# Stencil steps of a fused kernel: the row-neighbour products go into TensorE's PSUM sum, which becomes the new field

## The reference

```
ux = 0.5 * (jnp.roll(g, 1, axis=2) - jnp.roll(g, -1, axis=2))
vy = 0.5 * (jnp.roll(g1, 1, axis=3) - jnp.roll(g1, -1, axis=3))
...
D = 1.0 / (1.0 + 2.0 * Bx + 2.0 * By)
...
for _ in range(K):
    prev = h
    h = D * (c0 * h0 - 2.0 * E * h + cm_x * jnp.roll(h, 1, axis=2) + cp_x * jnp.roll(h, -1, axis=2) + cm_y * jnp.roll(h, 1, axis=3) + cp_y * jnp.roll(h, -1, axis=3))
    h = h + D * (2.0 * DT) * fsrc
    h0 = prev
return jax.nn.relu(_bn(h, out_gamma, out_beta, out_mean, out_var))
```

## Time and profile before

| what | value |
|---|---|
| median of 3 runs | 951.99 us (950.78 to 953.58) |
| the profiled execution, first to last instruction (its span) | 951.3 us |
| mean granted TensorE clock, as a share of full speed | 0.959 |
| matmul records, DVE instructions, POOL instructions | 3950, 671, 240 |

### The profile page before, as it was taken

How to read it: one execution, slowest core, us unless ns; L and a number is a source line. 1 busy time by engine, 2 the same in 40 slices (tenths; PEclk the granted TensorE clock), 3 DMA queues, 4 the chain that set the end, 5 groups by cost and what they waited for, 6 DMA issues and landing times. The chain is left out here.

```text
span 951.3 us, 10709 instructions
## 1 busy us (share of the span) xinstructions
PE 771.3 (81%) x3950; PEld 512.7 (54%) x3950; DVE 798.0 (84%) x671; ACT 552.9 (58%) x953; POOL 513.2 (54%) x240
## 2 busy tenths in 40 slices
PE   3999998987666778688799899898766677877895
PEld 2444443444366667678655444344435566866773
DVE  5899886269899898999989978725889999999983
ACT  3664332126758898889477433212484779888932
POOL 2005995020478697778410299901126969867841
PEclk8899999999899899999899999989998999999998
DMA  3000000000535345355200200000033445545521
GB/s 108 1 0 0 0 0 1 0 1 0 166 111 177 130 179 185 127 178 178 67 1 0 67 1 0 0 0 1 1 99 110 156 156 177 190 144 177 160 86 22
DMA packets 33296, 75.03 MB, mean 79 GB/s; under 512 B 15708, under 2 KB 15844, under 8 KB 33248
## 3 DMA queue, kind: packets, MB, share of 16 engines
q1 hardware_dynamic: 31840, 73.09, 23.2%
q0 software_dynamic: 320, 1.05, 0.5%
q10 hardware_dynamic: 1088, 0.26, 0.1%
HBM read 70.71 MB, written 2.62 MB: 77 GB/s over the span
## 5 line engine op out<-in xcount | busy, mean ns | idle before, releaser
L370 POOL TENSOR_TENSOR arena<-arena 128x1024 f32<-128x1024 f32 x127 | 300.7, 2381 | 92.7 <-DVE arena L1705 81.8
L1705 DVE TENSOR_TENSOR_SCAN arena<-arena,ps 128x1024 f32<-128x1024 f32 x128 | 289.4, 2280 | 19.2 <-ACT arena L931 11.4
L931 ACT ACTIVATE arena<-arena 128x128 f32<-128x128 f32 (+3 forms) x408 | 152.4, 448 | 86.2 <-DVE arena L1632 75.3
L931 ACT ACTIVATE arena<-arena,Amat 128x1024 f32<-128x1024 f32 x128 | 146.0, 1145 | 61.1 <-DVE arena L1705 60.4
L618 PE MATMUL ps<-mat,arena 128*128 128x128 f32 x1016 | 136.4, 279 | 3.3 <-POOL arena L370 2.5
L577 PE MATMUL ps<-mat,arena 128*128 128x128 f32 x560 | 79.1, 287 | 73.3 <-DVE arena L1705 58.6
L618 PEld LDWEIGHTS ps<-mat,arena 128*128 128x128 f32 x1016 | 119.0, 145 | 6.0 <-POOL arena L370 3.7
L577 PEld LDWEIGHTS ps<-mat,arena 128*128 128x128 f32 x560 | 63.3, 142 | 90.6 <-DVE arena L1705 74.2
L737 PE MATMUL ps<-arena,mat 128*128 128x512 f32 x240 | 106.3, 592 | 0.0
L931 ACT ACTIVATE arena<-ps 128x1024 f32<-128x1024 f32 (+2 forms) x65 | 56.1, 873 | 82.5 <-PE ps L449 23.6
L480 PE MATMUL ps<-arena,diag 128*128 128x512 f32 x180 | 83.0, 618 | 2.4 <-DVE ps L1543 2.4
(11 more groups left out here) (205 smaller groups left out, 1291.6 us busy)
## 6 DMA issues: line engine op xcount, KB each, us to landing
arena<-c_rows SPq DMA_DIRECT2D x128, 512.0 KB, 4.0
out<-arena SPq DMA_DIRECT2D x28, 64.0 KB, 2.3
xres<-x POOLq DMA_DIRECT2D x4, 256.0 KB, 5.5
xres<-x SPq DMA_DIRECT2D x4, 256.0 KB, 4.1
arena<-arena SPq DMA_DIRECT2D x4, 252.0 KB
convw<-conv_w SPq DMA_DIRECT2D x1, 576.0 KB
c_rows<-ROWS SPq DMA_DIRECT2D x4, 128.0 KB, 1.9
mat<-mats SPq DMA_DIRECT2D x1, 448.0 KB, 3.9
```

What stands on the lines that cost most here:

```text
L370: tt(HC[s % 2], HS[s % 2], CB[s % 4], ALU.mult).then_inc(S("hc"), 1)
L931: return nc.scalar.activation(out_, in_, func, bias=bias, scale=scale, accum_out=accum_out)
L1705: nc.vector.tensor_tensor_scan(HS[q], DA[q], PS[q][:, :], 0.0, ALU.mult, ALU.add).then_inc(S("scan"), 1)
```

## The change

PE adds two more terms: `R` and `XY` each go through the identity matrix into the same sum. The sum in PSUM is then the whole new field. POOL's add into `G1` and DVE's `new_h` are gone. The tile that holds the sum is the next step's field, and the tile that held the old field is seeded with the source for the next sum: the two tiles swap roles (`field_ps`). ACT copies the new field from PSUM to `hw` (`keep_field`) and no longer from `hw` to PSUM. The product with `P0` is made once per step in `products`, and steps 0 and 1 share the first one, which POOL makes; it lies in `g` or in `G1` by turns (`kept_product`). All loops over steps are written out instead of being hardware loops. At the end ACT's relu reads the sum's PSUM tile.

```diff
+        def field_ps(k, t):
+            return PS[2 * k + 1 - t % 2]
+
+        def kept_product(k, t):
+            return A[k]["g" if t < 2 or t % 2 else "G1"]
...
-                with pool.Fori(0, STEPS) as t:
+                for t in range(STEPS):
                     for k in range(2):
...
-                        pool.wait_ge(S("a_Q6"), 2 * h + k + 1)
-                        pool.wait_ge(S(f"a{k}_act"), 3 * it + 1)
-                        tt(img(a["R"]), img(a["Pmx"]), hw[:, :, 0:32], ALU.mult)
+                        if t == 0:
+                            pool.wait_ge(S("a_Q6"), 2 * h + k + 1)
+                        pool.wait_ge(S(f"a{k}_hw"), 2 * it + 2)
+                        tt(img(a["R"]), img(a["Pmx"]), hw[:, :, 0:32], ALU.mult).then_inc(S(f"a{k}_x"), 1)
                         tt(img(a["XY"]), img(a["G"]), hw[:, :, 2:34], ALU.mult).then_inc(S(f"a{k}_x"), 1)
-                        pool.wait_ge(S(f"a{k}_x"), 2 * it + 1)
-                        tt(a["G1"][:, :], a["R"], a["XY"], ALU.add).then_inc(S(f"a{k}_x"), 1)
...
+            def stencil_sum(h, k, t):
+                a, it, mix = A[k], STEPS * h + t, field_ps(k, t + 1)
+                pe.wait_ge(S(f"a{k}_seed"), 6 * h + t + 2)
+                pe.wait_ge(S(f"a{k}_g"), 4 * h + max(t, 1))
+                for n in range(2):
+                    mm(half(mix, n), ident, half(kept_product(k, t), n), start=False, stop=False, skip_group_check=True)
+                for name, count, mname, src in [("c", 2 * it + 1, "roll_up", "Pmy"), ("c", 2 * it + 2, "roll_down", "sden"), ("e", it + 1, "ident", "X"),
+                                                ("x", 2 * it + 1, "ident", "R"), ("x", 2 * it + 2, "ident", "XY")]:
+                    pe.wait_ge(S(f"a{k}_{name}"), count)
+                    for n in range(2):
+                        last = mm(half(mix, n), mt(mname), half(a[src], n), start=False, stop=(src == "XY"), skip_group_check=True)
+                last.then_inc(S(f"mix{k}"), 1)
...
+            def keep_field(h, k, t):
+                hw, field = wrapped(A[k]["hw"]), img(field_ps(k, t))
+                act.wait_ge(S(f"mix{k}"), STEPS * h + t)
+                av(hw[:, :, 1:33], field, ACT.Identity).then_inc(S(f"a{k}_hw"), 1)
+                act.wait_ge(S(f"a{k}_hw"), 2 * (STEPS * h + t) + 1)
                 av(hw[:, :, 0:1], hw[:, :, 32:33], ACT.Identity)
...
+            def seed(h, k, t):
+                if t == 0:
+                    act.wait_ge(S("a_Sc1" if k else "a_Sc"), h + 1)
+                if t >= 2:
+                    act.wait_ge(S(f"a{k}_g"), 4 * h + t)
+                av(field_ps(k, t + 1)[:, :], A[k]["Sc"], ACT.Identity).then_inc(S(f"a{k}_seed"), 1)
...
-                    act.wait_ge(S(f"a{k}_h"), (STEPS + 1) * h + STEPS + 1)
-                    av(img(PS[2 * k + 1]), wrapped(a["hw"])[:, :, 1:33], ACT.Relu, par[:, 4:5], par[:, 5:6]).then_inc(S("a_bnout"), 1)
+                    act.wait_ge(S(f"mix{k}"), STEPS * h + STEPS)
+                    av(field_ps(k, STEPS - 1)[:, :], field_ps(k, STEPS)[:, :], ACT.Relu, par[:, 4:5], par[:, 5:6]).then_inc(S("a_bnout"), 1)
...
+                else:
+                    dve.wait_ge(S(f"a{k}_hw"), 2 * (STEPS * h + t) + 1)
                 tt(img(a["Pmy"]), img(a["Kx"]), field, ALU.mult).then_inc(S(f"a{k}_c"), 1)
                 tt(img(a["sden"]), img(a["Ky"]), field, ALU.mult).then_inc(S(f"a{k}_c"), 1)
...
                 tt(img(a["X"]), img(a["Pe"]), field, ALU.mult).then_inc(S(f"a{k}_e"), 1)
...
-            def new_h(h, k, t):
-                a = A[k]
-                dve.wait_ge(S(f"mix{k}"), ONE + 2 * (STEPS * h + t + 1))
-                dve.wait_ge(S(f"a{k}_x"), 2 * (STEPS * h + t + 1))
-                tt(wrapped(a["hw"])[:, :, 1:33], img(PS[2 * k]), img(a["G1"]), ALU.add).then_inc(S(f"a{k}_h"), 1)
...
+                if 1 <= t < STEPS - 1:
+                    tt(img(kept_product(k, t + 1)), img(a["P0"]), field, ALU.mult).then_inc(S(f"a{k}_g"), 1)
...
+                for t in range(1, STEPS):
+                    products(h, 0, t)
+                    products(h, 1, t)
```

More of the change, by code:

```diff
@@ L253, in fused_blocks @@
         ONE = 1
[L254 removed]
+        PRIMED = ["y_read"]
         x_pix = x.rearrange("b (k q) w c -> b (q w) k c", q=4)
@@ L721, in _ @@
                 rolls(h, 1)
-                with pe.Fori(0, STEPS) as t:
+                for t in range(STEPS):
                     for k in range(2):
-                        a = A[k]
[L725 to L738, removed]
+                        stencil_sum(h, k, t)
                 group_mean(D[0], h, 1, 0)
@@ L1003, in from_D, with wrap, first_field @@
                     av(a["Sc"], a["Dc"], ACT.Identity, 2 * DT).then_inc(S("a_P0"), 1)
-            def wrap(h, k, t):
+            def wrap(h, k):
                 hw = wrapped(A[k]["hw"])
-                act.wait_ge(S(f"a{k}_h"), (STEPS + 1) * h + t + 1)
-                av(hw[:, :, 0:1], hw[:, :, 32:33], ACT.Identity)
[L1009 to L1020, removed]
+                act.wait_ge(S(f"a{k}_fri"), 5 * h + 5)
+                av(hw[:, :, 0:1], hw[:, :, 32:33], ACT.Identity).then_inc(S(f"a{k}_hw"), 1)
+                av(hw[:, :, 33:34], hw[:, :, 1:2], ACT.Identity).then_inc(S(f"a{k}_hw"), 1)
+            def first_field(k):
+                hc = wrapped(A[k]["hw"])[:, :, 1:33]
+                av(img(field_ps(k, 0)), hc, ACT.Identity).then_inc(S(f"a{k}_seed"), 1)
+            def keep_field(h, k, t):
[3 more added lines that the diff above has]
+                act.wait_ge(S(f"a{k}_hw"), 2 * (STEPS * h + t) + 1)
+                av(hw[:, :, 0:1], hw[:, :, 32:33], ACT.Identity)
+                av(hw[:, :, 33:34], hw[:, :, 1:2], ACT.Identity).then_inc(S(f"a{k}_hw"), 1)
+            def seed(h, k, t):
[4 more added lines that the diff above has]
+                av(field_ps(k, t + 1)[:, :], A[k]["Sc"], ACT.Identity).then_inc(S(f"a{k}_seed"), 1)
             def norm2(h, k):
@@ L1222, in _ @@
                     first_tap(h, 1, 1)
-                    wrap(h, 0, 0)
-                    wrap(h, 1, 0)
+                    wrap(h, 0)
+                    wrap(h, 1)
                     relu(h, 1, 0)
@@ L1239, in _ @@
                     for k in range(2):
-                        wrap(h, k, 0)
+                        wrap(h, k)
                 for k in range(2):
@@ L1247, in _ @@
                         act.wait_ge(S("a1_gg1"), 2 * h + 2)
-                        field(0)
+                        first_field(0)
                         act.wait_ge(S("a_Pe"), 2 * h + 1)
-                        seed(h, 0)
+                        seed(h, 0, 0)
                         from_D(h, 1)
@@ L1609, in minus_E, with products @@
                 tt(a["Pe"], a["Dc"], PS[2 * k][:, :], ALU.mult).then_inc(S("a_Pe"), 1)
[L1611 to L1617, removed]
+            def products(h, k, t):
+                a, field = A[k], img(field_ps(k, t))
+                if t == 0:
+                    dve.wait_ge(S(f"a{k}_seed"), 6 * h + 1)
+                    if h > 0 and k == 1:
+                        dve.wait_ge(S("stored1"), 128 * h)
+                else:
+                    dve.wait_ge(S(f"a{k}_hw"), 2 * (STEPS * h + t) + 1)
                 tt(img(a["Pmy"]), img(a["Kx"]), field, ALU.mult).then_inc(S(f"a{k}_c"), 1)
                 tt(img(a["sden"]), img(a["Ky"]), field, ALU.mult).then_inc(S(f"a{k}_c"), 1)
[L1620 removed]
+                if t == 0:
+                    dve.wait_ge(S("a_Pe"), 2 * h + k + 1)
                 tt(img(a["X"]), img(a["Pe"]), field, ALU.mult).then_inc(S(f"a{k}_e"), 1)
[L1623 to L1638 removed]
+                if 1 <= t < STEPS - 1:
+                    tt(img(kept_product(k, t + 1)), img(a["P0"]), field, ALU.mult).then_inc(S(f"a{k}_g"), 1)
             def add_stage0(h, k):
@@ L1770, in _ @@
                     x_neighbours(h, 1)
-                    previous(h, 0, 0)
-                    products(h, 1, 0, first=True)
+                    products(h, 1, 0)
                 if h == 0:
@@ L1780, in _ @@
                     products(h, 0, 0)
-                    previous(h, 0, 0)
                     products(h, 1, 0)
-                with dve.Fori(0, STEPS - 2) as t:
-                    step(h, t)
-                    previous(h, 0, t + 1)
-                    products(h, 1, t + 1)
-                step(h, STEPS - 2)
-                products(h, 1, STEPS - 1)
-                new_h(h, 0, STEPS - 1)
+                for t in range(1, STEPS):
+                    products(h, 0, t)
+                    products(h, 1, t)
                 add_stage0(h, 0)
-                new_h(h, 1, STEPS - 1)
                 group_norm(D[0], h, 1, 0)
```

27 lines of the change are left out of this document (8 added, 19 removed).

## The result

The changed kernel took 1012.09 us (median of 4 runs, 1009.68 to 1013.68). The kernel before took 952.79 us in the same session (4 runs, 950.78 to 953.76). The ratio is 1.0632, with a 95% interval of 1.0607 to 1.0657: slower by 6.3%. The forecast was 1015.4, with a range of 1009 to 1022. The profiled execution of the changed kernel has a span of 1011.6 us, 60.3 more than before; 63.4 had been forecast. It was the longest of the four runs (1013.68), so the medians, 59.3 apart, differ by a little less than the spans.

A forecast was written before the change was run, and what follows sets the result against it. PE, working without a gap, was taken to bound the stencil. Half 0's 33.3 us plus half 1's 30.7 less 0.6 for the convolution made 63.4; 951.3 + 63.4 = 1014.7, as a median 1015.4 us, range 1009 to 1022.

The forecast's parts named there:

- The added records: PE in the stencil: eight more matmul records per step of one pair, 10.30 us for 6.87, 34.3 us more per half.
- PE has room: Rival, stencil: others set PE's pace, so records could follow at 0.19 us; about 900 us in all; chance 3%.
- POOL and DVE, removed work: Stencil loop: POOL's 2.35 us add per pair and step and DVE's 13.6 us per half go, DVE's buying nothing inside.
- DVE pays for a part: Rival, stencil loop: DVE had set the pace, so its saved 13.6 us per half offsets PE's records; 993 us; chance 2%.
- The cover: Stencil: PE's 10.30 us on the other pair hides a pair's 5.9 us chain over ACT, DVE and POOL; cost nothing.
- PE waits or slows: Rival, stencil: PE at clock 0.959 gives about 1024 us, or waits cost 20 us per us each time; chance 7%.
- The copy for whose form there was no row: ACT's copy of the field from PSUM into inner columns of wide rows: taken as 1.0 us, bounds 0.98 and 1.25.
- The ends: Stencil ends: group mean read 0.32 us after its start, no longer held by `new_h`; halves 33.3 and 30.7 us longer.
- The stall of 0.1 us: Half 1's stencil start: PE's weights for `XY` come up just before POOL has made it; 0.1 us of waiting.
- The convolution: Behind each stencil half: first 18 records taken at 9.69 us in both halves, 0.6 us less than before in all.
- the clock holds behind the shorter gap: Rival, convolution behind the stencil: runs at full clock, 7.9 us per half; about 1011.8 us; a quarter of the forecast's chance.

The follow-up runs named there:

- run without the row terms: Changed kernel with PE leaving `R` and `XY` out of the sum, though POOL still makes them and PE waits for them: 952.05 us, ratio 0.999.
- group norm ahead: Kernel before, with DVE doing pair 0's whole group norm ahead of pair 1's last `new_h` behind the last stencil step: 949.56 us, ratio 0.9977.
- one term back to POOL: Changed kernel with POOL adding `R` into `XY` again and PE taking the sum as one term: 985.5 us, ratio 1.0355.
- two terms: Changed kernel with PE adding only the two rolled terms; the other four are made but left out: 906.29 us, ratio 0.951.

## Why the prediction was right

**The added records.** This step carried the forecast, and it held: 10.30 us per pair-step, 34.34 us more in half 0 from PE's start to the group mean. "PE has room" is refuted: 8 more records did not press the distance under 0.429, and the time followed the count at 16, 20 and 24 records, while at 8 POOL took over. The weight loads fill 45.60 of 103.00 us, 44% as before. The weight-load share, by which the prediction weighed TensorE's headroom (the Trainium skill, "Perfetto Trace Analysis", section "Identifying the Most-Contended Engine"), misleads for these float32 records: it was the same 44% with 160 and with 240 of them, and neither had room.

**POOL and DVE, removed work.** Right: nothing inside the loop. The run without the row terms kept half 0's 68.67 us with both engines relieved. "DVE pays for a part" is refuted by the same run.

**The cover.** "PE waits or slows" did not come: clock 1.00, no idle time of PE's matmuls in 206 us. The copy for whose form there was no row took 1.03 us against the 1.0 taken, and the seed had 7.7 us to spare against 7.8.

**The ends.** Half 0 was put at +33.3 and half 1 at +30.7; they came to +33.32 and +30.58. The read followed the group mean by 0.32 us, as forecast. The stall of 0.1 us at half 1's start reached only the weight load, which stood idle for 0.38 us instead of 0.24:

```profile
581.90 0.19 PEld L543 LDWEIGHTS ps<-arena,mat 128*128 128x128 f32 x1 [0.24 <-issue]
582.47 0.48 PEld L543 LDWEIGHTS ps<-arena,mat 128*128 128x128 f32 x2 [0.38 <-POOL arena L411]
```

It came 0.14 us late and still ahead of its matmul, so the matmuls lost nothing: the next pair-step began on the pitch, at 584.47 (574.17 + 10.30).

**The mis-sized terms.** The mechanism was right, and no large errors cancelled. The 3.1 us between forecast and measured span have three parts. The convolution was put at 9.69 us in both halves; it took 8.00 in half 0, where the clock held, and 9.69 in half 1. That is 1.7 us, and "the clock holds behind the shorter gap" came true in one half of two. Half 1's stencil gives 0.1. The other 1.3 lie where nothing was changed: the head (-0.6), the stage between the halves (-1.2) and the tail (+0.4). Executions differ there by as much without any cause in the code: written out alone, the kernel before began its stencil at 88.32 in place of 89.56, and had 385.08 us between the group mean of half 0 and half 1's stencil in place of 386.10. All of the -1.2 lies in half 0's stretch with those 52 steps (in the changed kernel 230.71 to 457.67): 226.96 us against 228.12 before. That stretch took 227.08 and 228.09 us in two runs of the kernel before whose edits do not touch it (loops written out, group norm ahead). So these parts are of the size of the spread; what makes the spread is not known. The range's lower end, by its own terms, is 1011.8 - 2 = 1009.8 and not 1009, which changes nothing here.

## What to carry to other kernels

Before an add is moved into PSUM as one more identity matmul, look whether TensorE has a gap in that very stretch. Here it had none, and a 128 x 1024 float32 term cost four records, 1.72 us, while DVE (about 1.13 us) and POOL (2.35 us) had done adds of the same size beside it. Where engines run side by side, what leaves the waiting ones pays only at the stage's ends, and there an exchange of two instructions in the order of an engine can bring it without the rest: here 0.2% (ratio 0.9977, 0.9966 to 0.9988).

## What was not expected of the hardware

Behind the same idle stretch of PE, 2.78 to 2.80 us, the same 18 records took 8.00 us once and 9.40 to 11.04 us nine times, one execution each of five kernels: the changed kernel (8.00, 9.69), one term back to POOL (9.69, 9.69), no row terms (9.69, 9.68), two terms (9.40, 11.04) and the group norm ahead (10.93, 10.63). What stood ahead of that stretch was not always as dense: in the run with two terms, and in half 1 of the group norm ahead, PE had idled there too. The windows of the convolution's first part in the changed kernel show that it goes with the clock (the last three columns are clock, DMA share and GB/s):

```profile
195.02:203.02 8.00, 8.00 (x21) 3.67 (x21) 2.94 (x5) 1.00 (x1) 0.00 (x0) 1.00 0.00 0
680.23:689.92 9.69, 9.69 (x21) 4.24 (x21) 2.94 (x5) 1.01 (x1) 0.00 (x0) 0.82 0.01 2
```

At 1.00 it is the full 2.4 GHz; 0.82 is a part at 1.2 GHz. The gap's length alone does not order the cost: before the change, gaps of 3.8 and 5.9 us cost no more (9.69 and 10.26 us) than these. With the gap filled, 0.70 to 1.05 us of it left, it was 7.99 or 8.00 in three of four cases, against one of ten without. That speaks for the idle stretch as the cause, but does not show it. Why the clock held once behind a gap of 2.79 us stays open.
